# Packing by ScalarE copies, state sums and the ninth tap over all 128 rows, outputs of a chunk's second half in PSUM partitions 64 to 127, and another item list

## The reference

```python
conv = conv_general_dilated(x, kernel)        # 9 taps, 64 -> 128 channels
v = conv * where(wnorm < 1, 1, 1 / wnorm)      # wnorm: norm of the 9-token window
h = relu(tanh(v) + bias)
# attention over layernorm(h), 8 heads of 16
q, k, v = split(layernorm(h) @ Wqkv + bqkv)
q, k = (elu(q) + 1) / 4, elu(k) + 1
memory = cumsum(outer(k * lam ** -t, v));  k_sum = cumsum(k * lam ** -t)
out = (q * lam ** t) @ memory / ((q * lam ** t) @ k_sum + eps)
h = h + layernorm(out @ Wout + bout) * gamma + beta
# 32 experts, each takes its best 371 of all 11872 tokens
G, idx = top_k(softmax(layernorm(h) @ W_router).T, 371)
h = h.at[idx].add(G * (silu(tokens[idx] @ W_up) @ W_down))
```

## Time and profile before

| | |
|---|---|
| median of 3 runs | 1230.74 us (1227.21 to 1232.94) |
| the profiled execution's own time | 1221.58 us |
| its span, first to last instruction | 1219.6 us |
| mean granted TensorE clock over the span | 0.835 |
| the 16 batches | from the start to about 777 us |
| search, then experts | to about 871 us, then to the end |

### The profile page before, as it was taken

How to read it: one execution, slowest core, us unless ns; L and a number is a source line. 1 busy time by engine, 2 the same in 40 slices (tenths; PEclk the granted TensorE clock), 3 DMA queues, 4 the chain that set the end, 5 groups by cost and what they waited for, 6 DMA issues and landing times.

```text
span 1219.6 us, 21893 instructions
## 1 busy us (share of the span) xinstructions
PE 945.5 (78%) x6489; PEld 754.6 (62%) x6489; DVE 668.7 (55%) x2137; ACT 381.3 (31%) x778; POOL 381.6 (31%) x338
## 2 busy tenths in 40 slices
PE   5498999999999999999999988200277677676772
PEld 4377788788787787777878867100155555555552
DVE  5354775676675676576667656588633233232320
ACT  0321332332432332333234232566332222222221
POOL 7020121121011011011111100000157777777775
PEclk9688988989998898898999878555578778787877
DMA  2112212212302302312230220100134444444432
GB/s 69 31 30 59 57 49 74 75 31 73 88 23 66 88 26 71 81 39 63 75 85 24 69 69 31 30 0 0 42 71 79 77 78 81 73 78 75 76 64 27
DMA packets 117085, 70.07 MB, mean 57 GB/s; under 512 B 40448, under 2 KB 113408, under 8 KB 117024
## 3 DMA queue, kind: packets, MB, share of 16 engines
q1 hardware_dynamic: 97568, 55.68, 17.1%
q0 software_dynamic: 19456, 13.74, 8.2%
HBM read 29.86 MB, written 20.23 MB: 41 GB/s over the span
## 4 chain that ended last, share of the span: by engine, by line
PE 44%; issue 15%; SPq 14%; POOL 10%; DMA 8%; DVE 7%; ACT 1%; DVEq 0%; POOLq 0%; ACTq 0%
SPq L394 12%; PE ps L807 8%; POOL out_dram L576 5%; PE pst L822 5%; PE po L844 5%; PE pa L755 4%; DMA f<-token_rows,idx 4%; PE po L928 3%; PE pc L868 3%; POOL f L566 3%; PE po L835 3%; DMA kd<-f 3%; PE pa L781 2%; SPq L400 2%; PE pa L757 2%
## 5 line engine op out<-in xcount | busy, mean ns | idle before, releaser
L576 POOL DMA_INDIRECT out_dram<-tqk,idx x96 | 154.1, 1605 | 48.6 <-issue 39.3
L807 PE MATMUL ps<-qb,kd 128*128 128x256 f32 x384 | 124.3, 452 | 37.7 <-DMA kd<-f 27.0
L566 POOL DMA_INDIRECT f<-token_rows,idx x96 | 96.1, 1001 | 85.9 <-issue 76.9
L755 PE MATMUL pa<-wc,xT 128*128 128x128 f32 x768 | 116.3, 297 | 6.6 <-DMA wc<-in_L_tok_kernel_dram 6.0
L928 PE MATMUL po<-qb 114*128 114x128 f32 (+1 forms) x576 | 111.6, 349 | 6.1 <-ACT qb L709 6.1
L755 PEld LDWEIGHTS pa<-wc,xT 128*128 128x128 f32 x768 | 97.7, 199 | 18.5 <-issue 9.1
L807 PEld LDWEIGHTS ps<-qb,kd 128*128 128x128 f32 x384 | 74.2, 215 | 55.4 <-issue 44.3
L530 POOL TENSOR_TENSOR wnorm<-wnorm,expo 128x6 f32<-128x6 f32 x16 | 21.1, 1321 | 278.3 <-DVE wnorm L1021 256.9
L928 PEld LDWEIGHTS po<-qb 114*128 114x128 f32 (+1 forms) x576 | 98.0, 250 | 9.2 <-ACT qb L709 7.8
L844 PEld LDWEIGHTS po<-vm,P 128*64 128x64 f32 x1536 | 103.7, 139 | 0.0
L844 PE MATMUL po<-vm,P 128*64 128x34 f32 x1536 | 103.5, 223 | 0.0
(11 more groups left out here) (230 smaller groups left out, 1964.7 us busy)
## 6 DMA issues: line engine op xcount, KB each, us to landing
token_rows<-row SPq DMA_DIRECT2D x16, 480.0 KB, 4.1
xT<-in_x_cols_dram SPq DMA_DIRECT2D x17, 388.0 KB, 4.3
vm<-sv SPq DMA_DIRECT2D x32, 204.0 KB, 3.5
qb<-f SPq DMA_DIRECT2D x256, 24.0 KB, 1.9
kd<-f SPq DMA_DIRECT2D x64, 96.0 KB, 2.4
out_dram<-h SPq DMA_DIRECT2D x16, 384.0 KB, 2.8
kd<-in_L_ffn_W_up_dram SPq DMA_DIRECT2D x32, 170.5 KB
...
```

The source lines that it names most:

```text
L566: eng.indirect_dma_start(out=xg[0:n, e.par, t, :], out_offset=None, in_=rows[:, :], in_offset=bass.IndirectOffsetOnAxis(ap=idx[0:n, e.k, t ...
L576: eng.indirect_dma_start(out=out_rows, out_offset=bass.IndirectOffsetOnAxis(ap=idx[0:n, e.k, t:t + 1], axis=0), in_=yw[0:n, e.par, t, :], ...
L755: eng.matmul(dst, xT[:, b.par, a:a + C], wc[:, t, :], start=(t == 0), stop=False)
L807: mm = eng.matmul(ps[c % 2][:, pack * 4 * HC:(pack + 1) * 4 * HC], kd[:, b.par, pack, c, :, :].rearrange("p u t -> p (u t)"), qb[:, b.par, ...
```

## The change

- **Packing.** The DMAs L394, L400 and L407 go. A new stage K of ACT copies does it for batch i-1: `dq0`, `dq1` copy half the tokens of q four times, each with a 0/1 column `turn_of` as scale (8 copies of 128x384 a batch, which write the zeros too), `dk` is 2 copies of 64x768, `dv` 4 copies of 64x408.
- **State sums.** `kt` gets a copy for each half with zeros in the other half's 64 rows (ACT's copy out of PSUM becomes two of 64 partitions), and the T matmul runs over all 128 rows.
- **Ninth tap.** `wc` gets 64 rows of zeros and the matmul runs over 128 rows.
- **V.** Half `u` of a chunk goes to partitions 64u to 64u+63 of `po`. `den` and `o` are 128 partitions by half the columns; the 12 transposes become 6 of 128 rows.
- **Start.** The `epst` pow and DVE's zeros for `qb` go; zeros for `kt` and four small instructions for `turn_of` come.
- **Item list.** A new `ORDER`, of which the diff shows the first line.

```diff
-        ORDER = [("A", "ts"), ("C", "o0"), ("A", "conv0"), ("T", 0), ("S", 0), ("A", "sq"), ("A", "win"), ("T", 1),
...
+        ORDER = [("A", "ts"), ("K", "dq0"), ("A", "sq"), ("C", "o0"), ("A", "conv0"), ("C", "o1"), ("T", 0),
...
-                batch = {"A": Batch(M, p), "S": before, "T": before, "V": before, "C": Batch(M - 1, p)}
+                batch = {"A": Batch(M, p), "K": before, "S": before, "T": before, "V": before, "C": Batch(M - 1, p)}
                 for stage, what in ORDER:
-                    if {"A": a, "S": b, "T": b, "V": b, "C": c}[stage]:
+                    if {"A": a, "K": b, "S": b, "T": b, "V": b, "C": c}[stage]:
...
-                if (stage, what) == ("A", "dq"):
...
-                    hold(eng, "f_done", b.count(4, 2))
-                    hold(eng, "s_ps", b.count(NC, NC, back=2))
-                    for h in range(H):
-                        g, j = h // 4, h % 4
-                        own = slice(E * h, E * h + E)
-                        for u in range(2):
-                            eng.dma_start(qb[own, b.par, u ^ g, j, :], f[own, b.par, 0, u, :]).then_inc(qb_in[b.par], 16)
-                if (stage, what) == ("A", "dk"):
-                    hold(eng, "f_done", b.count(4, 4))
-                    for g in range(2):
-                        own = slice(64 * g, 64 * g + 64)
-                        for u in range(2):
-                            eng.dma_start(kd[own, b.par, u ^ g, :, u, :], f[own, b.par, 1, :, :].rearrange(
-                                "p h (c u t) -> p (h c) u t", u=2, t=HC)[:, :, u]).then_inc(kd_in[b.par], 16)
...
-                if (stage, what) == ("A", "dv"):
-                    hold(eng, "vs_done", b.count(1, 1))
-                    hold(eng, "o_ps", b.count(NC, NC, back=2))
-                    for u in range(2):
-                        own = slice(HC * u, HC * u + HC)
-                        eng.dma_start(vm[own, b.par, :, u, :], sv[own, b.par, :, :, :].rearrange("p c h e -> p c (h e)")
-                                      ).then_inc(vm_in[b.par], 16)
...
-            eng.tensor_tensor(epst[:, :, :, :].rearrange("p s u h -> p (s u) h"),
-                              lam_row[0:HC, :].unsqueeze(1).to_broadcast([HC, 2 * SG, H]),
-                              esteps[:, :, :, :].rearrange("p s u h -> p (s u) h"), ALU.pow).then_inc(S["powers_done"], 1)
             eng.memset(kd[:, :, :, :, :, :], 0.0).then_inc(S["zero_done"], 1)
-            eng.memset(vm[:, :, :, :, :], 0.0).then_inc(S["zero_done"], 1)
+            eng.memset(vm[:, :, :, :, :, :], 0.0).then_inc(S["zero_done"], 1)
+            eng.memset(kt[:, :, :, :, :], 0.0).then_inc(S["zero_done"], 1)
...
+            step(eng.memset(head_of[:, :], 1.0))
+            step(eng.affine_select(out=head_of[:, :], in_=head_of[:, :], compare_op=ALU.is_ge, fill=0.0, base=0,
+                                   pattern=[[-E, H]], channel_multiplier=1))
+            step(eng.affine_select(out=head_of[:, :], in_=head_of[:, :], compare_op=ALU.is_ge, fill=0.0, base=E - 1,
+                                   pattern=[[E, H]], channel_multiplier=-1))
+            step(eng.tensor_tensor(turn_of[:, :], head_of[:, 0:4], head_of[:, 4:8], ALU.add))
...
-                    eng.activation(kt[:, b.par, lo:hi, :], pa[half][:, 0:(hi - lo) * D].rearrange("p (c d) -> p c d", d=D),
-                                   ACT.Copy).then_inc(S["kt_sb"], 1)
+                    for u in range(2):
+                        own = slice(HC * u, HC * u + HC)
+                        eng.activation(kt[own, b.par, lo:hi, u, :], pa[half][own, 0:(hi - lo) * D].rearrange("p (c d) -> p c d", d=D),
+                                       ACT.Copy).then_inc(S["kt_sb"], 1)
+                if stage == "K" and what in ("dq0", "dq1"):
+                    half = int(what[-1])
+                    cols = slice(half * QH, half * QH + QH)
+                    if first(b) and half == 0:
+                        eng.wait_ge(S["consts_pool"], ATTENTION_CONSTS)
+                    need(eng, "f_done", b.count(4, half + 1))
+                    need(eng, "s_ps", b.count(NC, HALF[half][1], back=2))
+                    for j in range(4):
+                        ins = eng.activation(qb[:, b.par, j, cols], f[:, b.par, 0, cols], ACT.Copy, scale=turn_of[:, j:j + 1])
+                    ins.then_inc(S["qb_done"], 1)
...
+                    for g in range(2):
+                        own = slice(64 * g, 64 * g + 64)
+                        ins = eng.activation(kd[own, b.par, :, :, g, :].rearrange("p c u t -> p (c u) t"),
+                                             f[own, b.par, 1, :].rearrange("p (n t) -> p n t", t=HC), ACT.Copy)
...
+                    for g in range(2):
+                        for u in range(2):
+                            ins = eng.activation(vm[64 * g:64 * g + 64, b.par, u, :, g, :],
+                                                 sv[HC * u:HC * u + HC, b.par, :, 4 * g:4 * g + 4, :].rearrange("p c h e -> p c (h e)"),
+                                                 ACT.Copy)
...
-                        mm = eng.matmul(dst, xT[CIN:128, b.par, a:a + C], wc[CIN:128, 4, :], start=False, stop=True)
+                        mm = eng.matmul(dst, xT[:, b.par, a:a + C], wc[:, 4, :], start=False, stop=True)
...
                 if stage == "S":
                     c = what
+                    if c in (0, HALF[1][0]):
+                        need(eng, "qb_done", b.count(2, 2 if c else 1))
                     if c == 0:
-                        need(eng, qb_in[b.par], b.m * 256 + 256)
-                        need(eng, kd_in[b.par], b.m * 64 + 64)
+                        need(eng, "kd_done", b.count(1, 1))
                     need(eng, "p_done", b.count(NC, c - 1))
-                    for pack in range(2):
-                        mm = eng.matmul(ps[c % 2][:, pack * 4 * HC:(pack + 1) * 4 * HC],
-                                        kd[:, b.par, pack, c, :, :].rearrange("p u t -> p (u t)"),
-                                        qb[:, b.par, pack, :, c * HC:(c + 1) * HC], start=True, stop=True)
+                    for u in range(2):
+                        n = c * C + u * HC
+                        mm = eng.matmul(ps[c % 2][:, u * 4 * HC:(u + 1) * 4 * HC],
+                                        kd[:, b.par, c, u, :, :].rearrange("p g t -> p (g t)"),
+                                        qb[:, b.par, :, n:n + HC], start=True, stop=True)
                     mm.then_inc(S["s_ps"], 1)
...
-                    eng.matmul(pst[:, 0:H * E1], kt[own, b.par, c, :], sv[own, b.par, c, :, :].rearrange("p h e -> p (h e)"),
+                    eng.matmul(pst[:, 0:H * E1], kt[:, b.par, c, u, :], sv[:, b.par, c, :, :].rearrange("p h e -> p (h e)"),
                                start=(k == 0), stop=True, skip_group_check=True).then_inc(S["st_ps"], 1)
...
-                            eng.matmul(po[0:HC, u * H * E1:(u + 1) * H * E1], f[:, b.par, 0, u, c * HC:(c + 1) * HC],
-                                       state[:, 2 * c + u, :], start=(u == 0 or c == 0), stop=False,
+                            eng.matmul(po[u * HC:(u + 1) * HC, 0:H * E1], f[:, b.par, 0, c * C + u * HC:c * C + (u + 1) * HC],
+                                       state[:, 2 * c + u, :], start=True, stop=False,
                                        skip_group_check=True)
...
-                    values = vm[:, b.par, c, :, :].rearrange("p u (g j e) -> p (u g) j e", g=2, j=4)
-                    outs = po[0:HC, 0:2 * H * E1].rearrange("p (a j e) -> p a j e", a=4, j=4)
-                    for pack, pair in enumerate((slice(0, 4, 3), slice(1, 3))):
+                    for u in range(2):
+                        outs = po[u * HC:(u + 1) * HC, 0:H * E1].rearrange("p (g j e) -> p g j e", g=2, j=4)
+                        values = vm[:, b.par, u, c, :, :].rearrange("p g (j e) -> p g j e", j=4)
                         for j in range(4):
-                            mm = eng.matmul(outs[:, pair, j, :], P[:, c % 2, pack, j, :], values[:, pair, j, :],
-                                            start=False, stop=(pack == 1 and j == 3), skip_group_check=True)
+                            mm = eng.matmul(outs[:, :, j, :], P[:, c % 2, u, j, :], values[:, :, j, :],
+                                            start=(c == 0 and u == 0 and j == 0), stop=(j == 3), skip_group_check=True)
...
-                        for u in range(2):
-                            dst, src = pc[half][:, k * C + u * HC:k * C + (u + 1) * HC], o[:, b.par, c, u * D:(u + 1) * D]
-                            if k == 0 and u == 0:
-
-                                eng.matmul(dst, src, ident[0:HC, 0:HC], start=True, stop=True)
-                            else:
-                                mm = eng.transpose(dst, src, ident[0:HC, 0:HC])
+                        mm = eng.transpose(pc[half][:, k * C:(k + 1) * C], o[:, b.par, c, :], ident[:, :])
...
```

(11 more changed lines are left out.)

88 lines of the change are left out of this document (47 added, 41 removed), and 22 rows, old and new, of the table ORDER.

## The result

The changed kernel takes 1025.40 us (median of 4 runs, 1022.96 to 1028.23), the kernel before, run beside it, 1231.84 us (4 runs, 1227.21 to 1247.12). The ratio is 0.8335 (95% interval 0.8298 to 0.8373). The profiled execution took 1024.46 us.

The account below looks back on a forecast made before the run. TensorE was taken to bound the batch part: 44.5 - 4.8 - 1.7 - 3.2 + 0.6 = 35.4 us an iteration. Over 15 iterations, 1221.6 - 136 - 4 = 1081, plus 4 gives 1085 us; range 1060 to 1138.

Parts of the forecast that it names:

- item 5: V in two partition halves: same records, same shape, so taken as 0 an iteration; drain from switching halves bounded at +3.6.
- lower bound of -1.2: V's two halves: 5 pairs of state-sum-like records running side by side would give 5 x 0.23 = -1.2 us.
- item 4: ACT's copies: mostly hidden, +0.6 us an iteration for first scores, `S 3` and smaller waits; bounds 0 and +4.
- that of two column halves: Rival for V: its two halves overlap instead of costing nothing or a drain; 1067 us or less, chance 0.10.
- Item 1: Ninth tap, state sums and transposes over 128 rows: 27 shape changes at 0.20 us go, -5.3; net -4.8 an iteration.
- without the overlap: Ninth tap and state sum starting together on different rows, at two places; losing this costs +0.5 us an iteration.
- The rule of the Trainium skill on row groups: Different row groups run together, so padding to 128 rows wastes array; rival: +2.5 instead of -4.8, 1195 us, chance 0.02.
- Items 2 and 3: TensorE's wait for `kd`'s DMA goes, -1.7 us, and the half-speed clock behind it, -3.2, in iterations with the fall.
- Item 6: DVE saves a little in `den` and `o`, but lies beside TensorE, so nothing was taken.
- Item 7: Kernel start: the `epst` pow, 8.0, goes; zeros for `kt` and four small instructions come: -4.3 us.
- The end: Last two iterations of the batch part, where TensorE is not full: taken as even.
- +4 to the median: Added to the profiled forecast of 1081, since the median of runs lay 9 us above the profiled execution.

## Why the prediction was wrong, point by point

The direction was right and so were the mechanisms but one; the gain came out 59.6 us larger than predicted. The step that failed is item 5, "V in two partition halves", taken as 0 with "it is the same shape".

- **Item 5.** Measured -2.6 us an iteration, 39 us over the 15, which came out 36 shorter than predicted. The lower bound of -1.2 counted only the pairs of 136 columns, 5 of them. Those came (0.51 to 0.28, five times; chunk 0 has a single one, which starts beside P times v of the other half, 316.61 and 316.62), and the records of P times v gave nearly as much again (1.01 to 0.80). With V's old form the iteration is 35.5 us against 35.4 predicted; it also holds 64-row transposes, which take 0.6 more than those of 128 rows, and has no wait, where item 4 had 0.6; that these two cancel is luck. I had the overlap of two row halves before me and gave that of two column halves 0.10.
 The Trainium skill, page "TensorE: Matmul & The Clock Gate", section on packing small matmuls, says that matmuls at different tile positions, rows or columns, run at the same time in one array. The traces agree for columns: 1.52 to 1.08, and to 0.82 when the halves alternate. I had weighed this page against the change for its rows and not used it for the change for its columns.
- **Item 1** (27 changes of shape, -4.8) holds in its unit price: 1.50 to 1.12 a chunk, 0.43 to 0.23 a state sum. Undone singly, tap and sums cost 25.7 and 36.7 us instead of 35 and 52, mostly because waits for `tsum` and other short ones go. With these waits added back, taps (2.2 us an iteration), sums (2.5 to 3.0) and transposes (0.6) give 5.3 to 5.8, where 5.3 was predicted without the overlap. That the overlap is worth something the kernel before showed: there the tap over 128 rows saves PE 1.3 us and not 2.3.
 The rule of the Trainium skill on row groups named there, which would have made 64-row sums free, does not show in this list: undone, the sums cost time.
- **Items 2 and 3** (-4.9): 4.7 by an iteration with a fall and one without in the kernel with k's DMAs on POOL, 4.0 as a mean of 15, since the kernel before had two iterations without a fall and the other kernel two with one. In the changed kernel the clock is 1.00 from 100 to 571 us. That this hangs on the wait alone isn't shown: the kernel with copies alone has a fall without a wait.
- **Item 4** (+0.6): 0.3 at `S 0` and 0.16 at `S 3`. What I did not see is DVE: a wait of 1.25 at the window sums in every second iteration. That the waits come out small hangs on the new list, to which the prediction gave no term; with the old one the same parts give 1073.01, by waits for ACT and DVE. So the prediction's silence on the list was harmless only because the list was good.
- **Item 6** (0): no run tests it by itself.
- **Item 7** (-4.3) missed that `S 0` of the second iteration waits 6.18 for `kd` (60.62, above). The pow came 4.6 earlier, where 4.3 was predicted, and the wait went too: -10.7.
- **The end**, "even", is -13.9. `S 0` at 540.92 waits 0.16 where it waited 5.72 (both lie ahead of this stretch), and behind it the clock stays up. In windows, before and after:

```profile
723.70:740.00 16.30, 15.41 (x78) 12.17 (x79) 6.31 (x15) 1.43 (x3) 1.52 (x2) 0.62 0.20 54
```

```profile
541.00:555.00 14.00, 12.17 (x118) 10.16 (x118) 12.09 (x44) 4.97 (x10) 1.95 (x3) 1.00 0.15 44
```

 At 0.62 over 16.3 us the clock took up to 6.2 us; the rest is not taken apart by a run. Undone singly, V in its old form adds 1.4 us to this stretch and the state sums over 64 rows 3.0.
- **+4 to the median**: measured +1.

The sum against the profiled execution: 1081 predicted, less 36 (iterations), 6.4 (start), 13.9 (end) and 0.2 gives 1024.5.
